# New orders for the first five pairs of an attention and expert block, and weight pieces split by two engines in turn

## The reference

```
qkv = x @ W_qkv + b_qkv;  q, k, v = split(qkv)
attn = softmax(q k^T / sqrt(128));  y = (attn v) @ W_out + b_out
x1 = layernorm(x + y)
h  = x1 + layernorm(x1)*g1+b1 @ attn_w^T
t  = layernorm(h)*g2+b2                        # 4096 tokens
logits = t @ gate_w^T;  the top 2 of 8 experts, rw = softmax(top 2)
for e in 8 experts:  out += comb[:, e] * ((silu(t @ gate_e^T) * (t @ up_e^T)) @ down_e^T)
result = layernorm(x1 + h + out)
```

## Time and profile before

| what | value |
|---|---|
| timed runs | 365.55, 367.7, 368.96 us |
| the profiled run, its own time | 366.52 us |
| its span, first to last instruction | 364.7 us |
| PE busy | 315.9 us (87%) |
| DVE, ACT, POOL busy | 255.6, 238.4, 210.9 us |
| mean granted clock of TensorE | 0.949 |

### The profile page before, as it was taken

The page is one execution under the profiler, slowest core; times in us unless marked ns, Lnnn a source line. Parts: engine busy times, 40 slices in busy tenths (PEclk is TensorE's granted clock), DMA queues, the critical chain, the costliest instruction groups (busy, mean ns, idle before and its releaser), DMA issues.

```text
span 364.7 us, 8735 instructions
## 1 busy us (share of the span) xinstructions
PE 315.9 (87%) x2052; PEld 273.7 (75%) x2052; DVE 255.6 (70%) x1031; ACT 238.4 (65%) x559; POOL 210.9 (58%) x251
## 2 busy tenths in 40 slices
PE   4859598749989989998999899899999999993970
PEld 3749487637878878987887788688888888872860
DVE  3385977797878869886988888866776666630660
ACT  2758655446776686776777677577777877750471
POOL 0394877848347656765587777676444443342760
PEclk9998788968999999999999999999999999996996
DMA  8266841143113121112112211332211111005931
GB/s 256 78 202 202 257 158 45 46 98 109 47 30 89 38 54 49 56 32 62 51 48 62 58 54 60 92 100 71 54 46 51 45 41 35 18 18 170 348 118 58
DMA packets 27872, 31.97 MB, mean 88 GB/s; under 512 B 4769, under 2 KB 21413, under 8 KB 27824
## 3 DMA queue, kind: packets, MB, share of 16 engines
q1 hardware_dynamic: 23504, 22.88, 20.8%
q0 software_dynamic: 4320, 8.53, 7.1%
HBM read 20.16 MB, written 11.68 MB: 87 GB/s over the span
## 4 chain that ended last, share of the span: by engine, by line
PE 67%; DVE 11%; issue 6%; ACT 5%; POOL 4%; DMA 3%; SPq 0%; POOLq 0%; ACTq 0%; DVEq 0%
PE bank L547 17%; PE bank L496 9%; PE bank L498 8%; PE bank L497 8%; PE bank L533 7%; POOL expert_rows L1331 3%; PE bank L449 2%; PE bank L557 2%; PE bank L697 2%; PE bank L433 2%; PE bank L691 2%; PE bank L410 2%; PE bank L411 1%; DMA w_raw<-weights 1%; PE bank L440 1%
## 5 line engine op out<-in xcount | busy, mean ns | idle before, releaser
L1340 POOL DMA_INDIRECT moe_rows<-ysb,xrow x71 | 70.4, 992 | 90.7 <-ACT ysb L768 84.6
L547 PE MATMUL bank<-wd,hidT 128*128 x568 | 76.4, 277 | 4.8 <-ACT t L775 3.9
L1331 POOL DMA_INDIRECT expert_rows<-rows,place x64 | 63.0, 985 | 20.7 <-issue 13.8
L547 PEld LDWEIGHTS bank<-wd,hidT 128*128 128x128 f32 x568 | 68.9, 192 | 7.6 <-issue 7.5
L496 PE MATMUL bank<-w_hi,t_hi 128*128 x142 | 63.1, 444 | 6.6 <-DVE t_lo L1179 3.1
L498 PE MATMUL bank<-w_hi,t_lo 128*128 x142 | 56.5, 398 | 0.0
L497 PE MATMUL bank<-w_lo,t_hi 128*128 x142 | 56.3, 397 | 0.0
L781 ACT ACTIVATE th<-bank 128x512 f32<-128x512 f32 x71 | 42.5, 599 | 16.6 <-PE bank L498 16.5
L1186 DVE SCALAR_TENSOR_TENSOR hid<-th,bank 128x512 f32<-128x512 f32 x71 | 48.3, 681 | 3.7 <-ACT th L781 3.7
L1190 DVE TENSOR_TENSOR hid<-hid,bank 128x512 f32<-128x512 f32 x71 | 48.8, 687 | 2.4
L1177 DVE CAST t_hi<-t 128x128 fp32r<-128x128 f32 x71 | 17.6, 248 | 45.7 <-ACT t L775 45.3
(11 more groups left out here) (158 smaller groups left out, 570.7 us busy)
## 6 DMA issues: line engine op xcount, KB each, us to landing
xrow<-expert_rows SPq DMA_DIRECT2D x71, 66.0 KB, 1.8
w_raw<-weights SPq DMA_DIRECT2D x16, 256.0 KB, 4.1
w_lo<-moe_rows SPq DMA_DIRECT2D x16, 256.0 KB, 5.5
xT<-xt SPq DMA_DIRECT2D x8, 256.0 KB, 4.3
wd<-weights SPq DMA_DIRECT2D x4, 512.0 KB, 8.7
out<-xs SPq DMA_DIRECT2D x16, 128.0 KB, 1.7
xs<-x SPq DMA_DIRECT2D x3, 512.0 KB, 7.1
moe_rows<-ysb,xrow POOLq DMA_INDIRECT x71, 2.3
```

The lines of the kernel that those rows point to most:

```text
L547: last = mm(ps_y, hidT[i % 2][:, c * P:(c + 1) * P], wd[:, bass.ds(w + c * P, P)], start=(c == 0), stop=(c == NC - 1))
L1331: G.indirect_dma_start(out=expert_rows[:, :], out_offset=bass.IndirectOffsetOnAxis(ap=place[:, i, k:k + 1], axis=0), in_=rows[:, i, k, :], ...
L1340: G.indirect_dma_start(out=moe_rows[:, :], out_offset=bass.IndirectOffsetOnAxis(ap=xrow[i % XR][:, C_DST:C_DST + 1].bitcast(I32), axis=0), ...
```

## The change

All engines get new orders for the fill. What can be told in words first, then the diff.

- **Splits.** DVE gets `split(i)` for the eight even pieces, with a semaphore wlo2_done; POOL keeps the eight odd ones. SP waits for piece i-4 on the semaphore of its parity. PE's first tile waits for 8 of each.
- **Order.** Pairs no longer advance as pairs; each batch's stages stand apart, and much of pair 1 moves ahead of pair 0's last stages. POOL's `second_root(2)` now stands behind `first_root(3)` and the last sends of pair 1. DVE's tail is now `x1_scale(3)`, `second_variance(2)`, `residual(9)`, `variances(4)`, `logits(2)`, `choose(2)`, `places(2)`.
- **Moved out of the loop.** `qk(10)`, `scores(10)`, `query_key(10)`, `turn_n1(3)`, `n1_turned(3)`, `attn_w(6)`, `attn_w(7)` and the last two `x1` of pair 3 now stand in the fill (`at(q, r, first)` skips them in the loop).
- **First four steps.** For q = 40 to 43 DVE runs `experts(q)` ahead of `early(q)`.

```diff
@@ SP
             def load_piece(i):
                 if i >= NWR:
-                    sp.wait_ge(sm["wlo_done"], i - NWR + 1)
+                    sp.wait_ge(sm["wlo_done" if i % 2 else "wlo2_done"], (i - NWR) // 2 + 1)
@@ PE, in experts(q)
-                        pe.wait_ge(sm["wlo_done"], B)
+                        pe.wait_ge(sm["wlo_done"], B // 2)
+                        pe.wait_ge(sm["wlo2_done"], B // 2)
@@ PE, front(q); likewise r = 1 (scores), 12, 13, 14; ACT r = 0, 11, 12, 13
-                g = at(q, 0)
+                g = at(q, 0, FILL + 1)
@@ PE, the fill (whole new order from the third batch)
+ qk(2) context(0) qk(3) scores(2) context(1) scores(3) turn_prob(2) values(2) values(3)
+ qk(4) turn_prob(3) context(2) context(3) qk(5) values(4) turn_n1(0) scores(4) attn_w(0)
+ attn_w(1) scores(5) turn_prob(4) values(5) qk(6) context(4) turn_n1(1) scores(6) rank(0)
+ turn_prob(5) values(6) attn_w(2) turn_prob(6) attn_w(3) qk(7) qk(8) context(5) context(6)
+ scores(7) values(7) scores(8) turn_prob(7) rank(1) turn_prob(8) values(8) context(7)
+ context(8) qk(9) turn_n1(2) scores(9) values(9) attn_w(4) attn_w(5) turn_prob(9)
+ context(9) qk(10) turn_n1(3) scores(10) attn_w(6) rank(2) attn_w(7)
@@ ACT, the fill (whole new order)
+ cast(2) cast(3) cast(4) query_key(2) cast(5) query_key(3) cast(6) softmax(2) cast(7)
+ cast(8) prob_turned(2) softmax(3) cast(9) values(2) values(3) prob_turned(3) cast(10)
+ x1(0, all) cast(11) query_key(4) values(4) n1_turned(0) query_key(5) cast(12) softmax(4)
+ cast(13) cast(14) prob_turned(4) cast(15) second_copy(0) x1(1, all) values(5) query_key(6)
+ n1_turned(1) softmax(5) gap_exp(0) softmax(6) prob_turned(5) values(6) prob_turned(6)
+ query_key(7) query_key(8) second_copy(1) values(7) softmax(7) gap_exp(1) softmax(8)
+ prob_turned(7) prob_turned(8) values(8) x1(2, all) query_key(9) n1_turned(2) values(9)
+ softmax(9) prob_turned(9) second_copy(2) x1(3, all) query_key(10) n1_turned(3) gap_exp(2)
@@ DVE
+            def split(i):
+                dve.wait_ge(sm["whi_done"], i + 1)
+                V.tensor_tensor(w_lo[:, :, cs], w_raw[i % NWR], w_hi[:, :, cs], ALU.subtract).then_inc(wlo2_done)
@@ DVE, the fill (whole new order, behind the copy of L1243)
+ split(0) split(2) split(4) residual(0) largest(2) split(6) residual(1) largest(3)
+ variances(0) split(8) x1_scale(0) residual(2) split(10) residual(3) variances(1)
+ largest(4) hidden(0) hidden(1) x1_scale(1) second_variance(0) split(12) split(14)
+ logits(0) largest(5) choose(0) residual(4) largest(6) places(0) hidden(2) hidden(3)
+ second_variance(1) residual(5) logits(1) largest(7) variances(2) choose(1) largest(8)
+ residual(6) places(1) x1_scale(2) plan_tiles(1) residual(7) residual(8) largest(9)
+ variances(3) hidden(4) hidden(5) x1_scale(3) second_variance(2) residual(9)
+ variances(4) logits(2) choose(2) places(2)
@@ DVE, the loop
-                early(q)
-                experts(q)
+                if q < STEADY + 4:
+                    experts(q)
+                    early(q)
+                else:
+                    early(q)
+                    experts(q)
@@ POOL, the fill (whole new order)
- split(0..5) first_root(0) split(6..12) second_root(0) first_root(1) split(13..15)
- send_rows(0, 0..2) first_root(2) send_rows(0, 3) second_root(1) send_rows(0, 4..7)
- send_rows(1, 0..7) second_root(2) first_root(3)
+ split(1) split(3) split(5) split(7) first_root(0) split(9) split(11) first_root(1)
+ split(13) second_root(0) split(15) send_rows(0, 0..3) second_root(1) send_rows(0, 4..5)
+ first_root(2) send_rows(0, 6..7) send_rows(1, 0..5) first_root(3) send_rows(1, 6..7)
+ second_root(2)
```

More of the change, by code:

```diff
@@ L289, in turn, with at @@
             return per * (i // n + 1)
-        def at(q, r):
+        def at(q, r, first=0):
             g, left = divmod(q - r - CHUNKS // 2, CHUNKS)
-            return g if left == 0 and 0 <= g < GROUPS else None
+            return g if left == 0 and first <= g < GROUPS else None
         def second(q, r):
@@ L856, in _ @@
             cast(3)
+            cast(4)
             query_key(2)
-            cast(4)
             cast(5)
@@ L895, in _ @@
             x1(1, 3)
+            values(5)
+            query_key(6)
             n1_turned(1)
-            query_key(6)
+            softmax(5)
+            gap_exp(0)
+            softmax(6)
+            prob_turned(5)
+            values(6)
+            prob_turned(6)
             query_key(7)
+            query_key(8)
             second_copy(1)
-            softmax(6)
+            values(7)
             softmax(7)
-            values(6)
-            values(7)
+            gap_exp(1)
+            softmax(8)
+            prob_turned(7)
+            prob_turned(8)
+            values(8)
             x1(2, 0)
@@ L1243, in _ @@
             V.tensor_copy(wa[:, D + E:D + 2 * E], banks[6][:, D:D + E]).then_inc(sm["wa_ready"], 1)
+            split(0)
+            split(2)
+            split(4)
             residual(0)
+            largest(2)
+            split(6)
             residual(1)
+            largest(3)
             variances(0)
-            largest(2)
+            split(8)
             x1_scale(0)
-            largest(3)
             residual(2)
+            split(10)
+            residual(3)
+            variances(1)
+            largest(4)
             hidden(0)
             hidden(1)
-            residual(3)
+            x1_scale(1)
             second_variance(0)
-            variances(1)
-            largest(4)
+            split(12)
+            split(14)
+            logits(0)
             largest(5)
-            logits(0)
             choose(0)
-            x1_scale(1)
+            residual(4)
+            largest(6)
             places(0)
-            residual(4)
-            residual(5)
-            variances(2)
             hidden(2)
             hidden(3)
-            largest(6)
             second_variance(1)
+            residual(5)
+            logits(1)
             largest(7)
+            variances(2)
+            choose(1)
+            largest(8)
+            residual(6)
+            places(1)
             x1_scale(2)
-            logits(1)
-            choose(1)
-            places(1)
             plan_tiles(1)
+            residual(7)
+            residual(8)
+            largest(9)
+            variances(3)
             hidden(4)
             hidden(5)
-            largest(8)
+            x1_scale(3)
             second_variance(2)
-            largest(9)
-            residual(6)
-            residual(7)
-            variances(3)
+            residual(9)
+            variances(4)
             logits(2)
             choose(2)
-            x1_scale(3)
-            residual(8)
-            residual(9)
             places(2)
-            variances(4)
             for q in range(STEADY, ALL):
-                early(q)
-                experts(q)
+                if q < STEADY + 4:
[4 more added lines that the diff above has]
+                    experts(q)
                 late(q)
```

158 lines of the change are left out of this document (76 added, 82 removed).

## The result

| | before | after | ratio (95%) |
|---|---|---|---|
| median of 20 runs each | 367.48 us (365.55 to 369.15) | 364.9 us (363.48 to 366.35) | 0.9928 (0.9915 to 0.9941) |
| the profiled run, its own time | 366.52 us | 363.73 us | |
| its span | 364.7 us | 361.8 us | |

The measured gain is 2.6 us, 0.7%. The time lies in the range (357 to 369) but outside my case (360 to 364), among the times forecast for "the loop gives it back". The sign held, the size did not.

A forecast was written before the change was run, and what follows sets the result against it. PE bounds the loop, a chain of waits over four engines the fill. S -0.45, POOL stretch +0.9, tail -4.3 and loop -1.7 gave 361.0 us for the profiled run, 362.0 as forecast median; range 357 to 369.

The forecast's parts named there:

- my case: Whole kernel: the main forecast, a time of 360 to 364 us, chance 0.45.
- the loop gives it back: Rival, first tiles: slow clock or waits for t32 lose 2 to 3 us, 365; chance 0.23 including late landing.
- S: Fill: the start of POOL's first send, forecast to move from 46.05 to 45.6 us.
- the stretch: Fill, POOL from first send to the end of second_root(2): 24.6 to 25.5 us, without a wait inside.
- The walk: Fill: step-by-step timing through the new queues, anchored at old rows, leading to the first send at 45.6 us.
- The splits on DVE: Fill: eight splits at 0.7 us where POOL is idle, some near 1.9 on meeting POOL's, at most 1.96.
- The bound of 4.7 us bought against 10.2: Fill: if every split pair runs serially, sharing splits saves 4.7 us of engine time instead of 10.2.
- the rival of the early places: Rival, fill: DVE meets few splits, the first send starts at 42, time 358 us; chance 0.17.
- The tail: From the end of second_root(2) to the first expert matmul: 11.5 to 7.2 us.
- the other sum: What remains behind second_root(2): 1.9 + 0.6 + 0.8 (places) + 3.1 (plan) + 0.8 (t_hi, t_lo, PE's start) = 7.2 us.
- Rows and plan: Before the first tile: t32 ready 6.2 us behind second_root(2), the plan 6.4, a tie within 0.2.
- Out of the loop: Loop: moving qk(10) and scores(10) into the fill takes 1.7 us off a full PE.

The follow-up runs named there:

- old_again: The kernel before, unchanged, run again for a second trace on a slower chip: 379.6 us against 379.44, ratio 1.0004.
- again_2: The changed kernel, unaltered, run again on a faster chip: 364.44 us against 367.43 for the kernel before, ratio 0.9921.
- again_3: The changed kernel, unaltered, run again on a faster chip: 364.08 us against 367.30 for the kernel before, ratio 0.9915.
- dve_splits_cut: The changed kernel with each of DVE's eight splits covering only 2 x 4 columns, the rest set to zero: 364.41 us, 0.9907 of before.
- places_first_2: The changed kernel with residual(4) behind places(0) on DVE, second run, on a faster chip: 363.94 us, 0.9917 of before.
- dve_early_first: The changed kernel with early(q) ahead of experts(q) in the first four steps too, on a slower chip: 379.18 us, 0.9974 of before.
- pair5_in_loop: The changed kernel with qk(10), scores(10) and query_key(10) back in the loop, on a slower chip: 379.53 us, 0.9978 of before.

## Why the prediction was right or wrong

**S, a step that failed: "45.6", measured 46.3 to 46.7.** With the stretch, the root ends at 72.1 on the mean instead of 71.1. Luck hid a part of the miss. The walk starts at the copy of L1243, at 16.29 before; forecast from there to S are 29.3 us, measured 31.18, 31.47 and 30.70. The copy itself came at 15.09, 15.22 and 15.98, and in old_again, with the old orders, at 15.06, so its moving isn't the change's work. On the way the walk was right on the whole but not in its parts. Forecast and measured (after): query_key(2) 20.5 and 19.38, softmax(2) 23.3 and 22.33, the end of variances(0) 25.9 and 25.75, hidden(0) 33.8 and 34.30, the end of places(0) 44.6 and 45.30. The step that went wrong is the one from softmax(2) to hidden(0): forecast 10.5 us, measured 11.97 (again_2 12.73, again_3 11.94). From hidden(0) to the end of places(0) it was 10.8 and 11.0.

The walk priced PE there at full speed. PE in order of time, after, and then again_3:

```profile
20.26 1.31 PE L433 MATMUL bank<-kT,qT 128*128 128x256 f32 x4 [2.48 <-ACT kT L720]
21.36 1.93 PE L449 MATMUL bank<-vo,probT 128*128 128x129 f32 x8
23.08 1.73 PE L433 MATMUL bank<-kT,qT 128*128 128x256 f32 x4
```

```profile
20.87 1.13 PE L433 MATMUL bank<-kT,qT 128*128 128x256 f32 x4 [2.20 <-ACT kT L720]
21.84 1.05 PE L449 MATMUL bank<-vo,probT 128*128 128x129 f32 x8
22.73 1.03 PE L433 MATMUL bank<-kT,qT 128*128 128x256 f32 x4
```

In after the scores that take 1.03 at 1.00 take 1.73, and the context 1.93 instead of 1.05: the level of 0.50. I had seen "PE has nothing else from 18.8 on" and charged only the gap. But that is not what made S late. In again_3 the same products ran at the full level (mean clock 1.00 from 20 to 25 us, 0.66 in after), the step took 11.94 us all the same, and S was 46.68. Counted from the copy S is 0.5 and 0.8 us sooner there than in the two other traces; that much at most may be the clock's.

Another thing is a meeting that I had counted on one side only. POOL in order of time, after:

```profile
25.82 2.01 POOL L1387 TENSOR_TENSOR r<-v,mhalf 128x8 f32<-128x8 f32 x1 [0.17 <-DVE v L1033]
...
37.71 1.38 POOL L1413 TENSOR_TENSOR r<-v,mhalf 128x4 f32<-128x4 f32 x1 [0.58 <-DVE v L1072]
```

first_root(0) takes 2.01 beside DVE's split(8), 1.67 elsewhere; second_root(0) 1.38 beside split(12) and (14), 1.04 elsewhere. In dve_splits_cut, where those splits are all but gone, they take 1.63 and 1.01. That is 0.34 us each on the way to S, and yet S from the copy stays (30.62 and 30.70), as said there. So 0.7 us of the overrun have a name, though taking them away buys nothing, and the rest stays open. The DVE side was right: x1_scale(0) (27.87, 1.23 us) and logits(0) (39.12, 1.25 us) each met a POOL split, as forecast. By the Trainium skill (SBUF — State Buffer, "Who interferes with whom") the engine that comes first holds the shared port pair for its whole instruction and the other is blocked. The DVE rows agree in size with a POOL split of 1.27 us; the POOL rows agree in that POOL is held too, but each time by 0.34 us, half of a DVE split's 0.68.

**The splits on DVE: 0.7 each, right; "some near 1.9", wrong.** The page's group has their mean.

```profile
L1002 DVE TENSOR_TENSOR w_lo<-w_raw,w_hi 128x512 fp32r<-128x512 f32 x8 | 5.4, 682 | 3.0 <-ACT w_hi L845 2.9
```

None of the eight met a POOL split in after; in seven of the variants one did (1.15 to 1.25 us), which is below my upper bound of 1.96. The bound of 4.7 us bought against 10.2 was the wrong question anyway: dve_splits_cut shows their time isn't on the path.

**The stretch, +0.9: right** (+0.95, no wait inside, places(1) in time) on the faster chips; on the slower one POOL waited 4.0 us in it. **The slack behind S was a missing thought**: places_first_2 shows that POOL waits at its roots if S alone comes sooner. Whether the rival of the early places (358), in which DVE's whole list would have come sooner, was to be had stays open; no trace has an S below 44.9.

**The tail, -4.3: nearly right** (-3.85). The forecast's own subtractions, 3.0 - 0.6 + 1.2 + 0.15 = 3.75, already led from 11.5 to 7.7, and 7.6 was measured. The 7.2 came from the other sum, whose 0.8 for t_hi, t_lo and PE's start was too small: measured 0.95, and 1.2 in before's own rows. rank(2) cost 0.63 (0.6 forecast). plan_tiles took 3.2 to 3.3 as said; logits to member took 2.0 and places with its copies a little more. Rows and plan did not tie: t32 was there at 76.95, 5.2 behind the root (6.2 forecast), the plan at 78.44. For the landing: tn started 5.2 behind the last send's start, where it had been 6.8.

**Out of the loop, -1.7: the step that failed most** (-0.6, 1.1 us short). The price of each product was right, and the effect of scores(10) is there in full: tile 2 to tile 3 takes 2.97 where it took 4.11, -1.14. But tile 1 to tile 2 takes 3.21 where it took 2.73, +0.48, although qk(10) is gone. "hidden(7) moves behind the first tile's hid ... nothing" was the error: hidden(6) and (7), 1.2 and 1.4 us of DVE, now stand behind t_hi and so in front of hid of tiles 0 and 1, and PE stands still for the second (1.00 us in after and again_2). dve_early_first measures it (0.9 us from the loop into the tail, the sum unchanged, see there for the clock), pair5_in_loop that qk(10) was nearly covered. I took 1.2 us off the tail and put it down nowhere. The clock isn't out of it: tile 0 to tile 1 takes 3.23 us in both kernels, at half clock in both, but in again_3 tile 1 too had the half level until 84.8. There PE waits for hid only 0.27 us, and the interval is 3.24 again:

```profile
86.30 0.49 PE L496 MATMUL bank<-w_hi,t_hi 128*128 x1 [0.27 <-DVE hid L1203]
```

The rival "the loop gives it back" came true in size (365), but that is partly luck: the loop gave back 1.1 us, by a wait that it didn't name, and S, the tail (0.45) and the end behind tile 70 the rest.

**The sign** came out of the tail: 3.85 us of DVE's work in another order, of which 0.9 come back in the loop. It is only kept because the shared splits bring back 2.2 of the 2.8 us that the new orders cost in S.

**Open.** Which of the first tile's two chains is the nearer on the faster chips once the plan is shortened; what the rest of the late S is; the 0.3 to 1.3 us behind tile 70; the slower chips' stall. No version beat the changed kernel by more than its interval.

## What to carry to other kernels

A piece of work that is moved off the path to the first tile keeps its duration: put it down where it lands, and look there for who waits for that engine, above all when the engine it lands in front of feeds a full PE. An earlier first item of an engine that works without gaps is worth only as much as the slack of everything it takes up later. Two halves of a change can each be worth nothing and the pair 0.8%: so undo halves in both directions before you name the cause.

## What the runs showed of the hardware that was not expected

- A POOL instruction of 4 or 8 columns was held up by a DVE instruction with two SBUF inputs: 2.01 instead of 1.67 us, 1.38 instead of 1.04, and 1.63 and 1.01 with the DVE instruction cut to 8 columns. Before, only DVE had been seen held.
- The same program has its first products of qk(1) at about 0.7 us in some runs and 1.19 in others, both for the kernel before and the changed one. The copy ahead of split(0) moved by 0.8 us with it (again_2 15.22, again_3 15.98), S not at all (46.69, 46.68): the run with the late copy had PE at the full level around 22 us, the one with the early copy at the half level.
- Two groups of chips give the same kernel 367.3 to 367.5 and 379.4 to 380.2 us, 3.4% apart. On the slower ones ACT stands still for up to 8.1 us in the fill with the new orders, put down to no engine, and the tiles 9 to 70 take 211 to 213 us instead of 204. The change was worth 0.7 to 0.85% on the faster and 0.3% on the one slower chip where it was measured.
